# Gathers issued in five bursts, a new order in the last pair, and one-hots of two tables per comparison, in a DLRM tower kernel

## The chip, the cores and the metric

The kernel runs on one core of a Trainium2 chip. The metric is the device time of one execution in microseconds (us), lower is better. In the profile the engines are PE (TensorE's matmuls), PEld (TensorE's weight loads), DVE (VectorE), ACT (ScalarE), POOL (GpSimd) and SP (SyncE).

## The reference, cut to what matters

For each of 2048 samples, 27 embeddings of 128 values are looked up in 27 tables, all pairs of them are multiplied (351 dot products), 16 context values are appended, and three dense layers follow.

```python
e = jnp.stack([tbl_0[ids[:, 0]], ..., tbl_26[ids[:, 26]]], axis=1)   # 2048 x 27 x 128
z = (e @ e^T)[:, i < j]                                              # 2048 x 351
h = concatenate([z, dense_ctx], axis=1)                              # 2048 x 367
h = maximum(h @ W_top1 + b_top1, 0)                                  # 512
h = maximum(h @ W_top2 + b_top2, 0)                                  # 256
y = h @ W_top3                                                       # 1
```

The tables have 1,000 to 125,000 rows. All is float32.

## The kernel before

The samples go in 8 pairs `p` of two tiles `t` of 128 samples. Pair 0 and pair 7 are written out, pairs 1 to 6 are one hardware loop (`sweep`). Every engine has its own program in that form, and semaphores tie them together.

The embeddings come in two ways. Ten tables of 1000 rows and one of 1250 stay in SBUF (`parts`, `x_parts`) and are looked up by matmul: VectorE makes one-hot columns by comparing the ids with row numbers (`make_onehot`, line 591, eight comparisons of 256 columns for one table), TensorE multiplies table and one-hot (`lookup`, line 697, two tables `k` at a time, five lookups of 32 matmuls; `lookup_x`, line 713). There are four one-hot buffers (`OH = 4`), so a one-hot waits until TensorE is through with the one four before it (`slot_free`). Semaphore `s_looked` counts first tables of a lookup, `emb_filled` counts finished PSUM banks.

The other 16 tables (numbers `n` = 0 to 15) are gathered by GpSimd: an indirect DMA per table and tile brings 128 rows (line 418), 32 gathers a pair (`x_rows` adds two in pair 0). They wait one for another (`one_queued`), for their buffer, and for a point of TensorE's program given by `keep_step`, which is asked once for each group of four. TensorE transposes the rows (`transpose_rows`, line 733), ScalarE or VectorE move them to `embT` (lines 463 to 471 and 597).

TensorE's order in pair `p` of the loop is: lookup 0, transpose of z of the pair before (tile 1), lookups 1 and 2, half of the first layer of the pair before (line 760), lookups 3 and 4, `lookup_x`, transposes of tile 0, rest of the first layer, gram 0, transposes of tile 1, second layer (line 774), gram 1, third layer (line 782), transpose of z of tile 0. A gram (`gram`, line 741) is 128 small matmuls, each a product of one sample's embeddings with themselves, which show as 256 matmul records and 256 weight loads. VectorE then turns the result (`flip`, line 603) and lays out z (`fill_z`). In pair 7 the dense layers of the last pair itself come in smaller steps (`LAST_LAYERS`, `last_rows`, lines 799 to 812).

The points that gathers wait for in the loop are, by groups of four: tile 0, n 0 to 3 none beyond the buffer; n 4 to 7 the end of tile 0's transposes of the pair before; n 8 to 11 its gram 0; n 12 to 15 its last transposes of tile 1. Tile 1: n 0 to 3 its gram 1; then the ends of lookups 0, 1 and 2 of this pair.

## Time and profile before

| | us |
|---|---|
| median of 3 runs (576.52 to 586.41) | 583.2 |
| profiled execution, its own time | 578.39 |
| its span in the profile | 576.6 |
| PE busy | 400.8 |
| DVE busy | 279.8 |
| POOL busy | 289.7 |
| mean granted TensorE clock | 0.828 of full |

The sums of the prediction are made against the profiled execution (578.39), which lies within the runs' spread and 0.8% under their median.

### The profile page before, as it was taken

To read this page: it belongs to the slowest core of one execution; us is meant where nothing else is said; L and a number is where in the kernel's file an instruction comes from. 1 tells how busy PE (TensorE), PEld (TensorE's weight loads), DVE (VectorE), ACT (ScalarE), POOL (GpSimd) and SP (SyncE) were. 2 spreads that over 40 slices of the span, in tenths; PEclk is the share of its full clock that TensorE was granted. 3 is DMA by queue.
4 is the path that set the end of the run, shared out by engine and by line. 5 is a ranking of instruction groups with operands and counts; after the bars stand their busy time and mean duration, and the time that the engine had idled before them with its cause. 6 is when DMAs were issued, how large, how long until landed. Compare 5 with 4: busy or idle time off the path is not lost.

```text
span 576.6 us, 15362 instructions
## 1 busy us (share of the span) xinstructions
PE 400.8 (70%) x6218; PEld 358.6 (62%) x6218; DVE 279.8 (49%) x804; ACT 142.1 (25%) x189; POOL 289.7 (50%) x264
## 2 busy tenths in 40 slices
PE   2756357877697365985778965796669926894865
PEld 2745347766596264875677853785549915794655
DVE  5673168774185341664427932555237904390210
ACT  2673111231132220222212411123102402132221
POOL 6673555534387553345426444484435974395000
PEclk9887558996798676888888977897679978798997
DMA  8984322121113112122121311221113221101000
GB/s 193 273 202 120 106 54 60 40 89 34 34 42 105 42 36 67 22 65 70 35 64 40 95 32 34 54 88 42 33 34 80 77 51 32 29 16 41 2 3 0
DMA packets 22295, 36.58 MB, mean 63 GB/s; under 512 B 12662, under 2 KB 13310, under 8 KB 22252
## 3 DMA queue, kind: packets, MB, share of 16 engines
q1 hardware_dynamic: 13996, 19.01, 12.1%
q0 software_dynamic: 8256, 16.92, 11.5%
q8 instruction: 36, 0.59, 0.4%
q14 instruction: 7, 0.06, 0.0%
HBM read 35.90 MB, written 0.01 MB: 62 GB/s over the span
## 4 chain that ended last, share of the span: by engine, by line
PE 58%; issue 25%; DVE 7%; another core or an unknown queue 5%; ACT 3%; DMA 2%; SPq 1%; DVEq 0%
PE emb_ps L697 22%; PE gram_ps L741 13%; PE emb_ps L733 5%; DVE onehot L591 5%; PE mlp_ps L760 5%; PE mlp_ps L774 4%; PE emb_ps L713 3%; DMA embT<-in_tbl 2%; PE mlp_ps L803 1%; PE mlp_ps L782 1%; PE mlp_ps L751 1%; PE mlp_ps L808 1%; ACT onehot L452 1%; DVE turned L603 1%
## 5 line engine op out<-in xcount | busy, mean ns | idle before, releaser
L418 POOL DMA_INDIRECT rows<-in_tbl,idx x256 | 287.3, 1122 | 238.2 <-PE gram_ps L741 81.8
L591 DVE TENSOR_SCALAR onehot<-ids_b,row_of 128x256 fp32r<-128x256 int32 x694 | 200.4, 365 | 69.1 <-remote 37.3
L697 PE MATMUL emb_ps<-onehot,parts 125*128 125x256 f32 x1280 | 177.4, 298 | 40.5 <-issue 37.9
L697 PEld LDWEIGHTS emb_ps<-onehot,parts 125*128 125x128 f32 x1280 | 168.6, 203 | 46.4 <-issue 43.0
L741 PE MATMUL gram_ps<-embT 128*32 128x26 f32 x4096 | 78.5, 223 | 103.0 <-issue 93.0
L741 PEld LDWEIGHTS gram_ps<-embT 128*32 128x32 f32 x4096 | 65.2, 144 | 119.8 <-issue 117.0
L603 DVE STREAM_TRANSPOSE turned<-gram_ps 128x832 f32<-128x832 f32 x16 | 16.8, 1050 | 149.3 <-PE gram_ps L741 149.3
L463 ACT ACTIVATE embT<-emb_ps 128x512 f32<-128x512 f32 x40 | 48.9, 1224 | 147.5 <-PE emb_ps L697 72.4
L471 ACT ACTIVATE embT<-emb_ps 128x512 f32<-128x512 f32 x32 | 36.9, 1226 | 105.1 <-PE emb_ps L733 94.1
L597 DVE COPY embT<-emb_ps 128x512 f32<-128x512 f32 x32 | 35.9, 1180 | 53.0 <-remote 29.4
L733 PE MATMUL emb_ps<-ident,rows 128*128 128x128 f32 x256 | 39.2, 312 | 13.0 <-ACT embT L467 11.6
L733 PEld LDWEIGHTS emb_ps<-ident,rows 128*128 128x128 f32 x256 | 34.5, 164 | 14.5 <-ACT embT L467 12.1
L760 PE MATMUL mlp_ps<-zT,w_sb 128*128 128x256 f32 (+1 forms) x168 | 42.5, 404 | 0.2 <-issue 0.2
L760 PEld LDWEIGHTS mlp_ps<-zT,w_sb 128*128 128x128 f32 (+1 forms) x168 | 33.4, 206 | 5.4 <-issue 0.6
L482 ACT ACTIVATE h<-mlp_ps,b_sb 128x256 f32<-128x256 f32 x42 | 17.5, 468 | 48.1 <-PE mlp_ps L760 15.6
L774 PE MATMUL mlp_ps<-h,w_sb 128*128 128x256 f32 x112 | 25.5, 379 | 0.9 <-issue 0.9
L713 PE MATMUL emb_ps<-onehot,x_parts 125*128 125x256 f32 x140 | 20.8, 299 | 5.5 <-issue 5.2
L713 PEld LDWEIGHTS emb_ps<-onehot,x_parts 125*128 125x128 f32 x140 | 19.3, 203 | 6.4 <-issue 6.3
L774 PEld LDWEIGHTS mlp_ps<-h,w_sb 128*128 128x128 f32 x112 | 20.7, 190 | 3.6 <-issue 1.0
L489 ACT ACTIVATE y<-mlp_ps 1x256 f32<-1x256 f32 x7 | 2.6, 374 | 61.6 <-PE mlp_ps L782 61.6
L475 ACT ACTIVATE zT<-mlp_ps 128x384 f32<-128x384 f32 x14 | 7.4, 526 | 14.2 <-PE mlp_ps L751 14.0
L618 DVE COPY z<-turned 128x351 f32<-128x351 f32 x16 | 9.4, 588 | 1.8 <-issue 0.2
(43 smaller groups left out, 112.7 us busy)
## 6 DMA issues: line engine op xcount, KB each, us to landing
ids_b<-in_ids_mm SPq DMA_DIRECT2D x8, 896.0 KB
ids_b<-in_ids_mm SPq DMA_DIRECT2D x16, 256.0 KB
rows<-in_tbl,idx POOLq DMA_INDIRECT x256
embT<-in_tbl SPq DMA_DIRECT2D x6, 448.0 KB
w_sb<-in_tbl SPq DMA_DIRECT2D x2, 448.0 KB
turned<-in_tbl SPq DMA_DIRECT2D x1, 560.0 KB
w_sb<-in_W_top SPq DMA_DIRECT2D x1, 512.0 KB, 4.7
turned<-in_tbl SPq DMA_DIRECT2D x1, 448.0 KB
```

Of the source, the lines that this page charges most:

```text
L418: pool.indirect_dma_start(rows[:, t, n, :], None, tables[f], bass.IndirectOffsetOnAxis(idx[:, t, f:f + 1], 0), engine_sem=gathers_written) ...
L463: nc.scalar.activation(*lookup_views(k), ACT.Copy).then_inc(emb_act, 1)
L471: nc.scalar.activation(*row_views(t, k), ACT.Copy).then_inc(emb_act, 1)
L591: last = nc.vector.tensor_scalar(onehot[:, k % OH, c, :], ids_b[:, of, :], row_of[:, first + c:first + c + 1], None, ALU.is_equal)
L597: nc.vector.tensor_copy(*row_views(t, k)).then_inc(emb_dve, 1)
L603: nc.vector.transpose(turned[:, 0:NJ * G], gram_ps[:].rearrange("p (g j) -> p j g", g=G)[:, 0:NJ, :]).then_inc(s_turned, 1)
L697: last = nc.tensor.matmul(emb_ps[BANK[k]][:, m * W:(m + 1) * W], parts[0:MP, f, part, c * D:(c + 1) * D], onehot[0:MP, f % OH, c, :], star ...
L713: last = nc.tensor.matmul(emb_ps[BANK[XJOB]][:, 0:W], x_parts[0:MP, part, at:at + D], onehot[0:MP, (NM + h) % OH, c, :], start=(h == part ...
L733: done = nc.tensor.transpose(bank[:, m * P:(m + 1) * P], rows[:, t, n, :], ident[:])
L741: last = nc.tensor.matmul(gram_ps[q * COLS:(q + 1) * COLS, g * COLS:g * COLS + NJ], embT[:, t, at:at + COLS], embT[:, t, at:at + NJ], star ...
L760: done = nc.tensor.matmul(mlp_ps[job % 2][:, m * W:(m + 1) * W], w1_sb[0:K1[c], c, n * P:(n + 1) * P], zT[0:K1[c], c, :], start=(c == 0), ...
L774: done = nc.tensor.matmul(mlp_ps[0][:, m * W:(m + 1) * W], w2_sb[:, n, m * P:(m + 1) * P], h1[:, n, :], start=(n == 0), stop=(n == N1 - 1))
```

## The change

Four things are changed. `keep_step` is asked before each gather, and waits at five places of a pair only, so that the 32 gathers run in bursts of 4, 7, 7, 7 and 7: tile 0's n 0 to 3 wait for gram 0 of the pair before; n 4 to 10 for its gram 1; tile 0's n 11 to 15 with tile 1's n 0 and 1 for the first table of lookup 1; tile 1's n 2 to 8 for the first half of the first layer; n 9 to 15 for the first table of lookup 4. Pair 0 has steps of its own. In pair 7 the order is z and transposes, then half of h1, half of gram 1, the other halves, h2; `LAST_LAYERS` follows that. After pair 0, `make_two` makes the one-hots of two tables with eight comparisons of 512 columns, and signals both at their end; it waits for both buffers at once.

```diff
-LAST_LAYERS = [(kind, t) for t in range(TILES) for kind in ("z", "h1", "h2", "y")]
+LAST_LAYERS = [("z", 0), ("h1", 0), ("h2", 0), ("z", 1), ("y", 0), ("h1", 1), ("h2", 1), ("y", 1)]
...
-            def keep_step(p, t, k):
+            def keep_step(p, t, n):
                 if isinstance(p, int) and p == 0:
...
+                    if (t, n) == (0, 8):
+                        pool.wait_ge(s_looked, looked(p, 0))
+                    elif (t, n) == (0, 13):
+                        pool.wait_ge(s_looked, looked(p, 1))
+                    elif (t, n) == (1, 0):
+                        pool.wait_ge(s_looked, looked(p, 2))
+                    elif (t, n) == (1, 5):
+                        pool.wait_ge(s_looked, looked(p, 3))
+                    elif (t, n) == (1, 10):
+                        pool.wait_ge(s_looked, looked(p, 4))
+                    else:
+                        return
+                elif (t, n) == (0, 0):
+                    pool.wait_ge(gram_filled, (p - 1) * TILES + 1)
+                elif (t, n) == (0, 4):
                     pool.wait_ge(gram_filled, p * TILES)
+                elif (t, n) == (0, 11):
+                    pool.wait_ge(s_looked, looked(p, 1))
+                elif (t, n) == (1, 2):
+                    pool.wait_ge(mlp_filled, (p - 1) * MLP_JOBS + 3)
+                elif (t, n) == (1, 9):
+                    pool.wait_ge(s_looked, looked(p, LOOK - 1))
                 else:
-                    pool.wait_ge(emb_filled, p * JOBS + k)
+                    return
                 pool.sem_inc(pool_waited, 1)
...
-                        keep_step(p, t, k)
                         for n in TR[k]:
                             f = GATHERED[n]
+                            keep_step(p, t, n)
                             one_queued((p * TILES + t) * NG + n + (TILES if first and t else extra))
...
+            def make_two(p, k):
+                dve.wait_ge(s_ids[ids_part(k)], (p + 1) * 16)
+                if k >= OH:
+                    slot_free(dve, p, k + 1 - OH)
+                else:
+                    held = NM if isinstance(p, int) and p == 1 else NE
+                    slot_free(dve, p - 1, [e for e in range(held) if e % OH == k + 1][-1])
+                for c in range(CH):
+                    last = nc.vector.tensor_scalar(onehot[:, k % OH:k % OH + LOOK_TABLES, c, :],
+                                                   ids_b[:, k:k + LOOK_TABLES, :], row_of[:, c:c + 1], None,
+                                                   ALU.is_equal)
+                last.then_inc(s_onehot, LOOK_TABLES)
...
                 if not first:
-                    for k in range(OH, NE):
-                        make_onehot(p, k)
+                    for k in range(OH, NM, LOOK_TABLES):
+                        make_two(p, k)
+                    for h in range(XHALVES):
+                        make_half(p, h)
                 if not last and not first:
-                    make_onehot(p + 1, 0)
-                    make_onehot(p + 1, 1)
+                    make_two(p + 1, 0)
...
-                    if not last and not first:
-                        make_onehot(p + 1, 2 + t)
+                    if not last and not first and t == 0:
+                        make_two(p + 1, LOOK_TABLES)
                     flip(p, t)
...
                 transpose_rows(p, 1, 1)
                 third_layer(p - 1)
                 last_layers("z", 0)
-                last_layers("h1", 0)
-                last_layers("h2", 0)
                 transpose_rows(p, 1, 2)
                 transpose_rows(p, 1, 3)
-                last_layers("y", 0)
+                last_layers("h1", 0, range(0, N1 // 2))
+                gram(p, 1, range(0, G // 2))
+                last_layers("h1", 0, range(N1 // 2, N1))
+                gram(p, 1, range(G // 2, G))
+                last_layers("h2", 0)
...
             sweep(pe, body)
-            for kind, t in LAST_LAYERS[4:]:
+            for kind, t in LAST_LAYERS[3:]:
                 last_layers(kind, t)
```

`make_half` is the old `make_onehot` for the two halves of the 1250-row table. ScalarE's program follows the same order.

## Rows read from the trace of the kernel before

**Rows 1.** The page, section 1: busy us, share of the span, instructions

```profile
PE 400.8 (70%) x6218; PEld 358.6 (62%) x6218; DVE 279.8 (49%) x804; ACT 142.1 (25%) x189; POOL 289.7 (50%) x264
```

**Rows 2.** The page, section 4: the chain that ended last, by engine

```profile
PE 58%; issue 25%; DVE 7%; another core or an unknown queue 5%; ACT 3%; DMA 2%; SPq 1%; DVEq 0%
```

**Rows 3.** Windows from a gram's start to its end: length, busy times, clock, DMA

```profile
125.10:136.74 11.64, 5.78 (x258) 4.29 (x258) 1.05 (x4) 0.84 (x2) 5.42 (x6) 0.68 0.16 42
...
461.41:480.94 19.53, 6.32 (x258) 4.96 (x258) 0.98 (x4) 0.84 (x2) 10.49 (x12) 0.65 0.17 41
...
sum 137.86, PE 62.78 PEld 51.70 DVE 16.28 ACT 9.35 POOL 59.54; mean PE 5.23 PEld 4.31 DVE 1.36 ACT 0.78 POOL 4.96
```

**Rows 4.** The same view: gram 0 of pair 7

```profile
536.86:539.22 2.36, 2.36 (x258) 2.32 (x258) 0.00 (x0) 0.84 (x2) 0.00 (x0) 1.00 0.03 7
```

**Rows 5.** Windows of pairs 1 to 6, gram 1's end to the next one's

```profile
356.78:431.11 74.33, 52.72 (x775) 46.46 (x774) 33.14 (x102) 15.29 (x19) 40.08 (x32) 0.81 0.19 50
...
sum 407.88, PE 295.38 PEld 265.15 DVE 207.97 ACT 88.73 POOL 214.83; mean PE 49.23 PEld 44.19 DVE 34.66 ACT 14.79 POOL 35.80
```

**Rows 6.** Windows of pairs 1 to 6, gram 1's end to gram 0's start

```profile
sum 234.87, PE 197.45 PEld 182.46 DVE 160.70 ACT 65.61 POOL 132.31; mean PE 32.91 PEld 30.41 DVE 26.78 ACT 10.93 POOL 22.05
```

**Rows 7.** Timelines of POOL and PE around gram 0 of pair 4

```profile
326.88 0.95 POOL L418 DMA_INDIRECT rows<-in_tbl,idx  x1 [6.75 <-PE emb_ps L733]
328.13 0.95 POOL L418 DMA_INDIRECT rows<-in_tbl,idx  x1 [0.30 <-DMA rows<-in_tbl,idx]
...
335.63 0.95 POOL L418 DMA_INDIRECT rows<-in_tbl,idx  x1 [0.30 <-issue]
342.20 0.95 POOL L418 DMA_INDIRECT rows<-in_tbl,idx  x1 [5.62 <-PE gram_ps L741]
...
329.65 0.54 PE L741 MATMUL gram_ps<-embT 128*32 128x26 f32 x39
...
338.35 2.87 PE L741 MATMUL gram_ps<-embT 128*32 128x26 f32 x205 [0.46 <-issue]
```

**Rows 8.** Windows of two runs of gathers, each cut where TensorE slows

```profile
243.57:251.56 7.99, 7.99 (x58) 7.60 (x57) 6.31 (x21) 2.13 (x4) 6.16 (x7) 1.00 0.18 47
...
342.20:347.00 4.80, 4.75 (x57) 3.95 (x55) 4.65 (x12) 2.27 (x4) 3.78 (x4) 1.00 0.17 41
...
251.56:254.99 3.43, 0.91 (x3) 0.52 (x4) 0.71 (x3) 0.00 (x0) 1.40 (x2) 1.00 0.19 48
```

**Rows 9.** Timeline of lookups beside gathers, pair 4

```profile
300.29 7.82 PE L697 MATMUL emb_ps<-onehot,parts 125*128 125x256 f32 x64
...
302.86 0.97 POOL L418 DMA_INDIRECT rows<-in_tbl,idx  x1 [2.09 <-remote]
...
314.34 11.94 DVE L591 TENSOR_SCALAR onehot<-ids_b,row_of 128x256 fp32r<-128x256 int32 x42 [3.62 <-remote]
...
314.50 1.21 ACT L463 ACTIVATE embT<-emb_ps 128x512 f32<-128x512 f32 x1 [8.88 <-remote]
```

**Rows 10.** Timeline of a gather beside one-hots, pair 5

```profile
367.65 12.17 DVE L591 TENSOR_SCALAR onehot<-ids_b,row_of 128x256 fp32r<-128x256 int32 x46
...
369.94 10.00 POOL L418 DMA_INDIRECT rows<-in_tbl,idx  x1 [7.48 <-PE emb_ps L697]
```

**Rows 11.** Windows of pair 0's grams and of pair 7

```profile
58.30:73.15 14.85, 5.83 (x257) 5.00 (x258) 1.49 (x1) 0.92 (x1) 7.57 (x8) 0.50 0.32 99
73.15:88.51 15.36, 8.59 (x274) 7.75 (x274) 9.02 (x22) 2.37 (x2) 7.72 (x8) 0.51 0.21 53
496.39:536.86 40.47, 32.71 (x230) 29.62 (x228) 20.64 (x64) 10.85 (x13) 25.55 (x16) 0.90 0.12 28
539.22:561.23 22.01, 15.15 (x339) 12.38 (x339) 4.25 (x6) 5.81 (x13) 0.00 (x0) 1.00 0.01 2
```

**Rows 12.** Timeline of the end, pair 7's gram 1 and h1

```profile
548.01 2.94 PE L803 MATMUL mlp_ps<-zT,w_sb 128*128 128x128 f32 x24 [0.58 <-ACT zT L497]
...
565.00 5.12 PE L803 MATMUL mlp_ps<-zT,w_sb 128*128 128x128 f32 x24 [0.58 <-ACT zT L497]
```

More of the change, by code:

```diff
@@ L544, in body @@
                                 layers(p - 1, 4)
-                                for kind, t2 in LAST_LAYERS[:3]:
-                                    last_layers(kind, t2)
+                                last_layers("z", 0)
                             move_rows(p, t, k)
-                    if last and t:
-                        last_layers(*LAST_LAYERS[3])
-                    elif not first:
+                    if not first and not (last and t):
                         layers(p - 1, 2 + t)
@@ L559, in _ @@
             sweep(act, body)
-            for kind, t in LAST_LAYERS[4:]:
+            for kind, t in LAST_LAYERS[1:]:
                 last_layers(kind, t)
@@ L577, in split_x_low, with make_onehot, make_half @@
                                         x_parts[0:MP, 0, :].bitcast(F32), ALU.subtract).then_inc(s_x_low, 1)
[L579 to L582 removed]
+            def make_onehot(k):
+                dve.wait_ge(s_ids[ids_part(k)], 16)
                 if k >= OH:
[L584 to L592 removed]
+                    slot_free(dve, 0, k - OH)
+                for c in range(CH):
+                    last = nc.vector.tensor_scalar(onehot[:, k % OH, c, :], ids_b[:, k, :], row_of[:, c:c + 1], None,
+                                                   ALU.is_equal)
+                last.then_inc(s_onehot, 1)
+            def make_two(p, k):
[3 more added lines that the diff above has]
+                else:
+                    held = NM if isinstance(p, int) and p == 1 else NE
+                    slot_free(dve, p - 1, [e for e in range(held) if e % OH == k + 1][-1])
+                for c in range(CH):
+                    last = nc.vector.tensor_scalar(onehot[:, k % OH:k % OH + LOOK_TABLES, c, :],
+                                                   ids_b[:, k:k + LOOK_TABLES, :], row_of[:, c:c + 1], None,
+                                                   ALU.is_equal)
+                last.then_inc(s_onehot, LOOK_TABLES)
+            def make_half(p, h):
+                slot_free(dve, p, NM + h - OH)
+                for c in range(XH):
+                    at = CH + h * XH + c
+                    last = nc.vector.tensor_scalar(onehot[:, (NM + h) % OH, c, :], ids_b[:, NM, :],
+                                                   row_of[:, at:at + 1], None, ALU.is_equal)
                 last.then_inc(s_onehot, 1)
@@ L734, in transpose_rows, with gram @@
                 done.then_inc(emb_filled, 1)
-            def gram(p, t):
-                past(pe, s_turned, p * TILES + t)
-                for g in range(G):
+            def gram(p, t, gs=range(G)):
+                if 0 in gs:
+                    emb_moved(p, t)
+                    past(pe, s_turned, p * TILES + t)
+                for g in gs:
                     for q in range(Q):
@@ L743, in gram @@
                                                 start=True, stop=True)
-                last.then_inc(gram_filled, 1)
+                if G - 1 in gs:
+                    last.then_inc(gram_filled, 1)
             def transpose_z(p, t):
@@ L784, in third_layer, with last_layers @@
                 done.then_inc(mlp_filled, 1)
-            def last_layers(kind, t):
+            def last_layers(kind, t, ns=range(N1)):
                 job, cols = LAST_LAYERS.index((kind, t)), bass.ts(t, P)
@@ L800, in last_layers @@
                 elif kind == "h1":
-                    for n in range(N1):
+                    for n in ns:
                         for c in range(KCH):
@@ L864, in body @@
                                 calls += 1
-                    emb_moved(p, t)
-                    gram(p, t)
+                        gram(p, t)
                 if not first and not last:
@@ L872, in _ @@
             sweep(pe, body)
-            for kind, t in LAST_LAYERS[4:]:
+            for kind, t in LAST_LAYERS[3:]:
                 last_layers(kind, t)
```

42 lines of the change are left out of this document (8 added, 34 removed).

## The prediction

> **What bounds the kernel now.** I read the page's busy shares first [rows 1]: TensorE is busy 70% of the span, no other engine over 50%. The chain that ended last [rows 2] is 58% TensorE and 25% "issue", that is, TensorE waiting for nothing that the profile shows. So the question is where TensorE, with work in hand, doesn't run. Windows laid on the grams answer it. The twelve grams of pairs 1 to 6 take 137.86 us, 11.5 each [rows 3]; the one gram that has no gather beside it, in pair 7, does the same 256 matmuls and 256 weight loads in 2.36 us [rows 4].
>
> The timelines of GpSimd and TensorE, side by side, show what is different. Gathers start every 1.25 us (326.88, 328.13). Eight of them run from 326.88 to 335.63 + 0.95 = 336.58. Gram 0 starts at 329.65, gets through 39 matmuls in 0.54 us, then almost stops until 338.35, where the other 205 go in 2.87 us [rows 7]. The next gathers start at 342.20, 1.0 us after that gram's end. Windows cut at the slowing give it a size [rows 8]: from the first gather of a burst on, TensorE gets through 58 + 57 records of lookups in 8.0 us in one case, and 57 + 55 of transposes, dense layer and gram in 4.8 us in the other; after that it makes 3 + 4 records in 3.4 us, until 254.99, 1.7 us after the end of the last of eight gathers (243.57 + 8 x 1.25 - 0.30 = 253.27). Five more bursts give counts of 53 to 63 each. So a burst costs TensorE nothing for its first 115 to 130 records, and nearly everything from there to 1.7 us after its end. Lookups need 7.6 us for 120 records, a gram less than one. That is why eight gathers are cheap beside lookups and dear beside a gram.
>
> A burst also keeps TensorE's signals back. The lookup that ends at 308.11 (300.29 + 7.82) is seen by ScalarE at 314.50 and the one-hots that wait for its first half start at 314.34, both 1.8 us after the burst's end (302.86 + 9.7 = 312.56); GpSimd's own condition is held too, so that bursts with a condition met meanwhile stand 2.09 us apart [rows 9].
>
> A pair takes 407.88 / 6 = 68.0 us [rows 5]: 234.87 / 6 = 39.1 from gram 1 to the next gram 0, the lookups above all [rows 6]; 23.0 in the two grams; the rest, (407.88 - 234.87 - 137.86) / 6 = 5.9, transposes of tile 1 and second layer.
>
> **The change part by part.** *Bursts, grams.* No condition lets a burst start just before gram 0; only the burst of four, which starts 1.0 us after gram 0, is near gram 1. Gram 0: 2.4 us. Gram 1: the four gathers start at +1.0 after gram 0, end at 1.0 + 4 x 1.25 - 0.3 = +5.7, let TensorE go at +7.4. TensorE reaches gram 1 at +5.9 with about 50 records made since the burst's start, makes 70 of 512, and the rest after +7.4 in 2.0: end +9.4, so gram 1 takes 3.5. Grams and what is between: 2.4 + 9.4 = 11.8 in place of 23.0 + 5.9 = 28.9, a gain of 17.1 a pair.
>
> *Bursts, lookups.* This is the cost. 28 gathers instead of mostly 16 now stand between gram 1 and gram 0, in four bursts of 7 x 1.25 - 0.3 = 8.45 us, more than the 7.6 us that TensorE has for free in lookups. The conditions are met while the burst before still runs (lookup 0 and a table of lookup 1 are 48 matmuls of 7.82 / 64 = 0.122 us [rows 9], 5.9, with some 2 us of third layer and transposes before them; the burst of seven ends at +9.5), so the next starts 2.1 us after its end. The chain is 1.0 + 4 x 8.45 + 3 x 2.1 = 41.1, + 1.7 until TensorE is let go, + 1.2 for the last move of transposed rows (the size of ScalarE's move in [rows 9]): 44.0. TensorE's own work there is 32.9 of 39.1 [rows 6], so GpSimd's chain ends later and sets it. Gathers back to back, without the 2.1s, would give 1.0 + 34.7 + 1.7 + 1.2 = 38.6, the lower bound.
>
> Two things come on top. *One-hots in twos*: same columns, same VectorE time if the time goes by columns: 46 comparisons of 256 columns take 12.17 us [rows 10], 0.264 each, so 0.53 for 512. But the first table of a lookup is signalled eight comparisons of 256, 2.1 us, later, and the one-hots now wait for a whole lookup. Behind the waiting comparison on VectorE are the other one-hots, the next moves of rows and `flip`; TensorE's next lookup waits for all. While VectorE is ahead by four buffers this is covered; after a burst that held the signals it isn't: 120 records are just the four buffers. I take 3 us a pair (one and a half such starts), 0 to 8 as ends (four starts). *Blocked gathers*: the gather at 369.94 takes 10.00 us while one-hots run without a break from 367.65 to 379.82 [rows 10]; there are four such (10.0 to 13.7 us) in the trace. Meanwhile TensorE runs free, as at 369.06. In the new chain GpSimd has less slack. 4 x 10.6 / 6 = 7 us a pair if all of it counts, 0 if none; I take 2, as the conditions behind it are then met and the gaps go.
>
> The stretch is then 44 + 3 + 2 = 49 in place of 39.1, a loss of 9.9. A pair: 49 + 11.8 = 60.8 against 68.0, 7.2 less; six pairs: -43.
>
> *Pair 0* [rows 11]. Gram 0 of 14.85 us loses its eight gathers (the steps of pair 1 wait for its end) but the last burst of pair 0 now starts later, so I leave it 3: -12. From there to gram 1's end 15.4 becomes 9.4: -6.
>
> *Pair 7* [rows 11]. Its stretch of 40.47 becomes 49: +8.5; gram 0 was clean already. The new order puts the last transposes into the wait for ScalarE's zT and h1 and the gram into the waits around it: the chain from gram 0's end to gram 1's end, 22.0 us, loses h2 (16 matmuls, 16 x 2.94 / 24 = 2.0 us), y, and the waits of TensorE for h1, h2 and the moved rows: between -2 and -8, I take -5. H1 of tile 1 takes 5.12 at the end against 2.94 earlier [rows 12], its clock granted at half after a wait; -1 for a part of that. Sum -6.
>
> Sum: 578.4 - 43 - 18 + 8.5 - 6 = 520 us, 10% under the profiled time.
>
> **Two rules of the Trainium skill.** The row of one-hots shows 0.264 us for 256 columns [rows 10]. The Trainium skill, VectorE: DVE Perf Modes, section on the TRN2 errata, says that operations from SBUF pay a fixed cost per instruction, 58 cycles, and should be 512 elements or wider. By that rule, 40 comparisons fewer would save an estimated 2.4 us of VectorE a pair, and the sum would be some 515; start to start, the trace shows no such cost. The same group shows a gather blocked through a run of one-hots. The Trainium skill, SBUF — State Buffer, section "Who interferes with whom", says that a VectorE instruction with one SBUF input, outside the two-port modes, doesn't contend with GpSimd. By that rule the blocks would not come, and the stretch would be 47, the sum 506; the trace disagrees with the 10.00 us.
>
> **The rivals.** *The bursts are covered* (12%). The stretch stays at about 39 to 43: TensorE's 120 free records reach nearly through a burst, and half a first layer in a burst, with fewer records per us, stretches them. For it: clean bursts of four, and pair 6 did the stretch in 461.41 - 431.11 = 30.3 us [rows 3, 5]. Against it: GpSimd's chain of 38.6 to 44.0 is there in any case. At 41: 6 x 8 less, 520 - 48 - 8 = 464.
>
> *Holds cost more than they free, but not all* (18%). Each of four holds is followed by one-hots that start from empty buffers (2.1 to 4.3 us) and by lookups at half clock. Stretch 53 to 57: +6 us for each of seven, 520 + 42 = 562.
>
> *The blocked gather becomes the bound* (10%, the other side). A gather that meets a run of one-hots waits for the run's end. Now bursts start just as VectorE gets its signals back, so each of three bursts in the lookups can meet one, and comparisons are twice as long. At 10.6 us and no cover, the stretch is 44 + 3 + 10.6 n for n blocks a pair. The gain of 17.1 is used up at a stretch of 56.2, n = 0.9; with n = 1.4 it is 62, a pair takes 74, and the whole 520 + 7 x 13 = 611. It decides from about one counted block a pair; the trace has 0.6, mostly covered. Pair 5, with one, is the longest at 74.33 [rows 5]; pair 6, with one, has a gram of 19.5 us [rows 3].
>
> *The conditions don't hold the gathers off the grams* (part of the above): if the last burst starts later than its point, gram 0 waits for its end. This costs nothing beyond the 44.0, which already waits for it.
>
> **How the numbers follow.** The forecast, stretch of 44 to 53, gives 485 to 548 and has 60%. The rivals have 12, 18 and 10. The range of 474 to 566 leaves out about half of the first and all of the last, with a little between. A difference under 2% can't be told from none here. Faster by over 2% (under 571.5): 0.60 + 0.12 + most of 0.18 = 0.84. Within 2%: 0.09. Slower by over 2%: 0.07.
>
> **What the profile of the changed kernel would show.** Gram 0 at 2.4 to 5 us and gram 1 at 3 to 5 in pairs 1 to 6. Gathers in runs of 4, 7, 7, 7, 7 with 2.1 us between. The time from gram 1 to gram 0 at 44 or more, its end set by the last burst. TensorE stopping in lookups some 7.6 us into a burst, then VectorE's one-hots starting 1.7 us after the burst. One-hots of 512 columns 0.53 us apart. Wrong would be: grams still at 10 us; gathers of 10 us twice in each pair; a stretch over 56.

## The result, and the profile after

| | before, us | after, us |
|---|---|---|
| median of the runs | 583.1 (576.5 to 586.4) | 509.0 (506.3 to 517.7) |
| profiled execution, its own time | 578.39 | 506.26 |
| its span | 576.6 | 504.3 |

The ratio is 0.875, 95% interval 0.864 to 0.885: faster by 12.5%. The profiled execution lost 72.1 us. All of this holds for the chip on which both kernels were measured here. On the one other chip on which the whole change was timed, the kernel before takes 431 us and the change makes it 12 us (3%) slower, and half of the experiments are about that.

The page after, sections 1 and 4 (engine busy times; the chain that ended last, by engine), answers to [rows 1] and [rows 2]:

```profile
PE 384.9 (76%) x6218; PEld 347.5 (69%) x6218; DVE 236.6 (47%) x524; ACT 142.7 (28%) x189; POOL 273.0 (54%) x264
PE 57%; issue 15%; another core or an unknown queue 13%; DVE 6%; DMA 3%; ACT 3%; SPq 1%; DVEq 0%
```

Waiting for nothing visible ("issue") fell from 25% to 15% of the chain. Waits put down to "another core or an unknown queue" rose from 5% to 13%: the kernel runs on one core, and in the timeline below such waits (there `remote`) are signals that arrive late. VectorE's work fell by 43.2 us with 280 comparisons fewer.

Windows of pairs 1 to 6. First the grams, two of the twelve and the sum [rows 3, 4]:

```profile
111.51:116.21 4.70, 2.99 (x257) 2.57 (x258) 2.85 (x8) 0.84 (x2) 0.24 (x1) 1.00 0.08 21
...
175.53:177.88 2.35, 2.35 (x257) 2.31 (x258) 2.35 (x8) 0.00 (x0) 0.00 (x0) 1.00 0.06 6
...
sum 52.50, PE 34.05 PEld 31.19 DVE 14.42 ACT 8.38 POOL 9.53; mean PE 2.84 PEld 2.60 DVE 1.20 ACT 0.70 POOL 0.79
```

Then from one gram 1's end to the next one's [rows 5], and from gram 1's end to gram 0's start [rows 6]:

```profile
127.66:186.70 59.04, 45.97 (x776) 42.13 (x774) 27.36 (x62) 14.94 (x19) 34.36 (x32) 0.91 0.21 61
...
sum 356.07, PE 283.14 PEld 258.03 DVE 169.82 ACT 88.76 POOL 206.13; mean PE 47.19 PEld 43.01 DVE 28.30 ACT 14.79 POOL 34.36
...
69.20:111.51 42.31, 34.49 (x227) 32.08 (x227) 24.04 (x58) 10.78 (x12) 29.89 (x28) 0.85 0.27 77
...
sum 271.26, PE 216.79 PEld 198.69 DVE 130.53 ACT 67.02 POOL 176.94; mean PE 36.13 PEld 33.11 DVE 21.75 ACT 11.17 POOL 29.49
```

The grams gave back 137.86 - 52.50 = 85.4 us; the stretches between took 271.26 - 234.87 = 36.4 more; what is left of the pairs gained 2.8. Six pairs: -51.8.

The timeline of the burst of seven after gram 1 of pair 1 shows the price (start, length, engine, line, work; in brackets the idle time before it and what ended it; [rows 7, 9, 10] are its like before):

```profile
128.65 0.94 POOL L427 DMA_INDIRECT rows<-in_tbl,idx  x1 [6.74 <-PE gram_ps L766]
128.77 4.03 PE L720 MATMUL emb_ps<-onehot,parts 125*128 125x256 f32 x32
...
132.89 2.02 PE L720 MATMUL emb_ps<-onehot,parts 125*128 125x256 f32 x15
...
135.80 0.64 PE L720 MATMUL emb_ps<-onehot,parts 125*128 125x256 f32 x4 [0.89 <-issue]
...
137.27 0.52 PE L720 MATMUL emb_ps<-onehot,parts 125*128 125x256 f32 x3 [0.83 <-issue]
...
138.78 6.42 DVE L605 TENSOR_SCALAR onehot<-ids_b,row_of 128x512 fp32r<-128x512 int32 x16 [8.79 <-remote]
...
139.92 1.05 POOL L427 DMA_INDIRECT rows<-in_tbl,idx  x1 [2.83 <-remote]
...
141.27 4.05 POOL L427 DMA_INDIRECT rows<-in_tbl,idx  x1 [0.30 <-issue]
142.09 5.56 PE L720 MATMUL emb_ps<-onehot,parts 125*128 125x256 f32 x32 [2.05 <-DVE onehot L605]
```

TensorE stops at 134.9, 6.3 us into the burst. The burst ends at 137.09 (its last gather starts at 136.15 and takes 0.94), VectorE and GpSimd get their signals 1.7 and 2.8 us later, and TensorE then waits 2.05 us for two whole tables of one-hots. The gather beside those one-hots takes 4.05 us and ends with them (141.27 + 4.05 = 145.32; 138.78 + 6.42 = 145.20).

Where a burst is still running when gram 0 is due, gram 0 pays. In pair 2 the last gather has ended (171.95 + 0.94) and gram 0 starts 2.6 us later; in pair 4 gram 0 starts with the last two gathers still to end, and takes 5.22 us:

```profile
171.95 0.94 POOL L427 DMA_INDIRECT rows<-in_tbl,idx  x1 [0.30 <-issue]
...
291.48 0.43 PE L766 MATMUL gram_ps<-embT 128*32 128x26 f32 x27
292.58 1.28 POOL L427 DMA_INDIRECT rows<-in_tbl,idx  x1 [0.30 <-issue]
293.12 0.18 PE L766 MATMUL gram_ps<-embT 128*32 128x26 f32 x1 [1.21 <-issue]
...
294.55 2.15 PE L766 MATMUL gram_ps<-embT 128*32 128x26 f32 x227 [0.53 <-issue]
```

Windows of pair 7's stretch, its gram 0, from there to gram 1's end, and the rest [rows 11, 12]:

```profile
425.27:470.20 44.93, 36.79 (x231) 32.76 (x228) 17.44 (x40) 12.01 (x15) 28.13 (x28) 0.89 0.17 42
470.20:475.15 4.95, 2.78 (x257) 2.62 (x257) 0.00 (x0) 0.00 (x0) 0.00 (x0) 0.93 0.03 7
475.15:491.44 16.29, 13.99 (x322) 11.77 (x320) 4.24 (x6) 5.15 (x10) 0.00 (x0) 0.92 0.01 2
491.44:504.30 12.86, 8.62 (x67) 7.22 (x67) 2.09 (x4) 3.41 (x11) 0.00 (x0) 1.00 0.00 1
```

### The profile page after: what moved, and what is told of

It is laid out like the page before. It is cut to its first block, busy times and chain, and to the rows that moved or that the text cites. A ratio compares the mean times of both kernels' runs of the same rounds, so it can differ in the third digit from the quotient of the medians.

```text
span 504.3 us, 15021 instructions
## 1 busy us (share of the span) xinstructions
PE 384.9 (76%) x6218; PEld 347.5 (69%) x6218; DVE 236.6 (47%) x524; ACT 142.7 (28%) x189; POOL 273.0 (54%) x264
## 4 chain that ended last, share of the span: by engine, by line
PE 57%; issue 15%; another core or an unknown queue 13%; DVE 6%; DMA 3%; ACT 3%; SPq 1%; DVEq 0%
PE emb_ps L720 25%; PE gram_ps L766 10%; PE mlp_ps L786 6%; PE emb_ps L756 5%; PE mlp_ps L800 5%; PE emb_ps L736 4%; DMA embT<-in_tbl 3%; DVE onehot L605 3%; DVE turned L627 1%; DVE embT L621 1%; PE mlp_ps L829 1%; SPq L272 1%; ACT onehot L461 1%; PE mlp_ps L777 0%
## 5 line engine op out<-in xcount | busy, mean ns | idle before, releaser
L427 POOL DMA_INDIRECT rows<-in_tbl,idx x256 | 270.7, 1058 | 192.0 <-PE gram_ps L766 68.9
L720 PE MATMUL emb_ps<-onehot,parts 125*128 125x256 f32 x1280 | 195.5, 309 | 66.4 <-issue 48.1
L720 PEld LDWEIGHTS emb_ps<-onehot,parts 125*128 125x128 f32 x1280 | 179.9, 212 | 76.8 <-issue 56.8
L605 DVE TENSOR_SCALAR onehot<-ids_b,row_of 128x512 fp32r<-128x512 int32 x280 | 114.8, 485 | 77.3 <-remote 46.1
L766 PE MATMUL gram_ps<-embT 128*32 128x26 f32 x4096 | 48.8, 199 | 36.8 <-issue 27.0
L766 PEld LDWEIGHTS gram_ps<-embT 128*32 128x32 f32 x4096 | 43.7, 116 | 45.3 <-issue 40.4
L615 DVE TENSOR_SCALAR onehot<-ids_b,row_of 128x256 fp32r<-128x256 int32 x70 | 21.9, 379 | 57.6 <-remote 51.7
L756 PE MATMUL emb_ps<-ident,rows 128*128 128x128 f32 x256 | 35.3, 293 | 3.5 <-ACT embT L476 3.1
L736 PE MATMUL emb_ps<-onehot,x_parts 125*128 125x256 f32 x140 | 27.4, 360 | 6.8 <-issue 6.6
L736 PEld LDWEIGHTS emb_ps<-onehot,x_parts 125*128 125x128 f32 x140 | 25.5, 271 | 9.8 <-issue 9.8
L591 DVE TENSOR_SCALAR onehot<-ids_b,row_of 128x256 fp32r<-128x256 int32 x64 | 20.2, 386 | 5.3 <-DMA ids_b<-in_ids_mm 5.3
```

The source lines that it names most:

```text
L427: pool.indirect_dma_start(rows[:, t, n, :], None, tables[f], bass.IndirectOffsetOnAxis(idx[:, t, f:f + 1], 0), engine_sem=gathers_written) ...
L605: last = nc.vector.tensor_scalar(onehot[:, k % OH:k % OH + LOOK_TABLES, c, :], ids_b[:, k:k + LOOK_TABLES, :], row_of[:, c:c + 1], None, A ...
L615: last = nc.vector.tensor_scalar(onehot[:, (NM + h) % OH, c, :], ids_b[:, NM, :], row_of[:, at:at + 1], None, ALU.is_equal)
L720: last = nc.tensor.matmul(emb_ps[BANK[k]][:, m * W:(m + 1) * W], parts[0:MP, f, part, c * D:(c + 1) * D], onehot[0:MP, f % OH, c, :], star ...
L736: last = nc.tensor.matmul(emb_ps[BANK[XJOB]][:, 0:W], x_parts[0:MP, part, at:at + D], onehot[0:MP, (NM + h) % OH, c, :], start=(h == part ...
L756: done = nc.tensor.transpose(bank[:, m * P:(m + 1) * P], rows[:, t, n, :], ident[:])
```

## The experiments

Each later kernel was timed beside the kernel before on its own chip, and the first thing seen was that the kernel before takes 430 us on five chips and 570 on two. The table gives medians in us, and the chip by its number.

| label | chip | before | kernel | ratio, 95% interval |
|---|---|---|---|---|
| e1_bursts_only | 11 | 430.1 | 438.4 | 1.020 (1.009 to 1.030) |
| e2_wide_only | 11 | 430.1 | 426.9 | 0.995 (0.987 to 1.004) |
| e3_order_only | 11 | 430.1 | 421.9 | 0.984 (0.978 to 0.990) |
| e5_twos_of_256 | 11 | 430.1 | 428.7 | none given |
| e0_after (the change itself) | 12 | 431.4 | 443.3 | none given |
| e6_no_gathers | 12 | 431.4 | 387.1 | none given |
| e4_after_single_tables | 1 | 432.3 | 422.4 | 0.980 (0.967 to 0.993) |
| e7_one_burst_of_28 | 1 | 432.3 | 437.0 | 1.013 (1.003 to 1.024) |
| e8_order_and_wide | 10 | 431.7 | 420.4 | 0.973 (0.965 to 0.980) |
| e10_bursts_only_again | 0 | 430.1 | 440.9 | 1.026 (1.016 to 1.035) |
| e9_no_wait_for_gram_1 | 13 | 568.7 | 558.4 | 0.981 (0.975 to 0.988) |
| e11_no_wait_for_gram_1_again | 15 | 571.5 | 556.7 | 0.972 (0.960 to 0.983) |

Three medians say less than they seem to. On chip 12 one of eleven runs of the kernel before took 414.6 us and the others 427.4 to 434.6. One run of e5 took 416.4 and the other three 428.0 to 429.5; its trace is of the 416.4. The four runs of e10 lie between 431.2 and 455.7; its trace is of the 431.2.

### One part of the change at a time

e1_bursts_only is the kernel before with the new `keep_step` alone:

```diff
-                        keep_step(p, t, k)
                         for n in TR[k]:
                             f = GATHERED[n]
+                            keep_step(p, t, n)
```

> The kernel before with the five bursts alone. Theory A (the gain is gathers taken off the grams): 515 to 530 us, grams of pairs 1 to 6 at 2.4 to 6 us, the stretch from gram 1 to gram 0 at 45 to 48. Rival B (the wide comparisons carry a large part): 545 us or more, the grams short all the same.

e2_wide_only is the kernel before with `make_two` and `make_half` alone:

```diff
-                    for k in range(OH, NE):
-                        make_onehot(p, k)
+                    for k in range(OH, NM, LOOK_TABLES):
+                        make_two(p, k)
```

> The kernel before with the one-hots of two tables alone. Theory A: 575 to 585 us, within 2% of before, since the grams stay at 10 to 12 us. Rival B: 560 or less.

e3_order_only is the kernel before with the new `LAST_LAYERS` and `last_rows` alone:

```diff
-LAST_LAYERS = [(kind, t) for t in range(TILES) for kind in ("z", "h1", "h2", "y")]
+LAST_LAYERS = [("z", 0), ("h1", 0), ("h2", 0), ("z", 1), ("y", 0), ("h1", 1), ("h2", 1), ("y", 1)]
```

> The kernel before with the new order of the last pair alone. Theory A: 5 to 9 us less than before in the span after gram 0 of pair 7, so 574 to 578 in all. Rival B: nothing, because the last chain is set by gram 1 and h1 of tile 1.

e5_twos_of_256 is the changed kernel with each comparison of 512 columns as two of 256, the signal still for two tables:

```diff
-                for c in range(CH):
-                    last = nc.vector.tensor_scalar(onehot[:, k % OH:k % OH + LOOK_TABLES, c, :],
-                                                   ids_b[:, k:k + LOOK_TABLES, :], row_of[:, c:c + 1], None,
+                for m in range(LOOK_TABLES):
+                    for c in range(CH):
+                        last = nc.vector.tensor_scalar(onehot[:, k % OH + m, c, :], ids_b[:, k + m, :],
+                                                       row_of[:, c:c + 1], None,
```

> The kernel after, but each comparison of 512 columns made as two of 256; both tables are still signalled together. The trace after shows 0.396 us from one 512-wide comparison to the next, 0.263 for 256 before, that is 0.13 fixed and 0.52 ns a column. Theory C (the width counts): one-hots of two tables take 4.2 us in place of 3.2, and TensorE waits for them after each burst, some three starts a pair: 520 to 530 us. Rival D (only the number of signals or the burst holds count): 506 to 512.

The times expected for all four were those of a chip like the first, and all four missed: on this one the kernel before took 430.1 us. What they show is what the parts are worth where a gram isn't stopped. Windows of the grams of pairs 1 to 6 in e3_order_only, whose gathers stand where they stood before:

```profile
148.88:152.76 3.88, 3.51 (x258) 2.92 (x258) 1.04 (x4) 0.84 (x2) 2.96 (x4) 1.00 0.19 53
...
sum 55.94, PE 41.91 PEld 35.23 DVE 15.20 ACT 10.10 POOL 42.50; mean PE 3.49 PEld 2.94 DVE 1.27 ACT 0.84 POOL 3.54
```

There are 42.50 us of gathers beside them, where [rows 3] had 59.54, and still a gram takes 4.7 us and not 11.5; one with four gathers beside it takes 3.88. So there four gathers beside a gram cost some 1.5 us together (3.88 - 2.36), and the bursts have little to gain: alone they lose 2%, the order alone gains 8 us, the wide one-hots 3, which can't be told from nothing (the interval goes from a gain of 6 to a loss of 2).

### Is it the chip, and is it the gathers?

e0_after is the changed kernel unaltered, to see it on such a chip.

> The changed kernel itself, beside the kernel before once more. On the chip of the four runs so far the kernel before takes 430 us, and its grams take 3.8 to 6 us with gathers beside them. Theory E (a burst of gathers holds TensorE on some chips only, and the change pays there alone): where before takes 575 to 590, after takes 500 to 520; where before takes 425 to 435, after takes 420 to 440, since the bursts cost 8 us there, the order gains 7 and the wide comparisons 2. Rival F (the hold is there on every chip, and the 430 us have another cause): a ratio of 0.86 to 0.89 wherever it runs.

e6_no_gathers is the kernel before with the gathers and the loads of their indices left out after pair 0. TensorE transposes pair 0's rows again in every pair, so 7 of 8 pairs compute with the wrong embeddings for 16 of the 27 tables.

```diff
                 extra = 0 if first else TILES
+                if not first:
+                    return
...
-                        load_idx(p + 1, t)
...
-                pe.wait_ge(s_rows[t][k], (p + 1) * 16 * len(TR[k]))
+                pe.wait_ge(s_rows[t][k], 16 * len(TR[k]))
```

> The kernel before, with all gathers and index loads left out after pair 0 (TensorE transposes the rows of pair 0 again, so the results of later pairs are not the reference's). Theory E: where before takes 575 to 590, this takes 400 to 420, all grams of pairs 1 to 6 at 2.4 to 5 us; where before takes 430, it takes 390 to 415. Rival F: about 410 in both.

On chip 12 the changed kernel took 443.3 us and the kernel before 431.4: the two differ by 12 us, the other way than at first, so the rival that expected 0.86 to 0.89 everywhere is out. (Both kernels fell just outside what had been expected: 443.3 against 420 to 440, 387.1 without gathers against 390 to 415.) The changed kernel's pairs, from one gram 1's end to the next, sum to 311.36 us against 356.07 on the first chip, and 18 of the 45 us lie in TensorE's busy time, at a granted clock of 0.90 to 0.94 against 0.86 to 0.92; the other 27 are stops that aren't there. Without gathers the pair is 247.56 / 6 = 41.3 us and every gram in the loop from pair 2 on takes 2.35 or 2.36. So even here the gathers of the kernel before cost 431 - 387 = 44 us, and on the first chip nearly 200, if the rest takes as long there.

The gathers themselves don't tell the chips apart. Their packets of 4096 bytes took 248 ns on average in the kernel before on the first chip, 247 in e3_order_only on chip 11; 240 in e9_no_wait_for_gram_1 on chip 13 and 238 in e0_after on chip 12. On each of the seven chips all runs of the kernel before are of one kind, but for one single run of 518 us on chip 1, at a granted clock of 0.653, of which there is no trace. But each of the seven was used in one sitting only, and the number of the first chip isn't known. So whether the kind belongs to the chip, or to something that lasts for a sitting, wasn't tried; "chip" in this text stands for both. What makes the difference isn't shown by any of these runs.

### What costs the change 12 us on the other chips

e4_after_single_tables is the changed kernel with the old one-hots, one table at a time (bursts and order alone). e7_one_burst_of_28 is the changed kernel without the three conditions within the lookups, so that after gram 1 all gathers go one behind the other.

```diff
-                elif (t, n) == (0, 11):
-                    pool.wait_ge(s_looked, looked(p, 1))
-                elif (t, n) == (1, 2):
-                    pool.wait_ge(mlp_filled, (p - 1) * MLP_JOBS + 3)
-                elif (t, n) == (1, 9):
-                    pool.wait_ge(s_looked, looked(p, LOOK - 1))
```

> The kernel after with one-hots of one table per comparison and per signal, as before: bursts and order alone. Where before takes about 430 us (gathers don't hold TensorE): bursts alone took 438 and the order alone 422, so 430 by the sum of parts; theory G (the wide comparisons cost time there, because one signal for two tables and a wait for both buffers delay the lookup) says 425 to 432, under the 443 of the whole; rival H (the bursts are what costs, the width nothing) says 438 to 445. Where before takes about 583 us: 505 to 520.

> The kernel after without the three conditions inside the lookups: after gram 1 the 28 gathers go in one run, held by their buffers alone. Where gathers hold TensorE (before at 583): after 115 to 130 records TensorE would stop until the run ends, 28 us later, so the stretch from gram 1 to gram 0 is 60 or more and the whole 600 or more. Where they don't (before at 430): the last rows of tile 1 land earlier, TensorE doesn't wait for them, and the whole is 425 to 435, under the 443 of the kernel after.

e8_order_and_wide is the kernel before with both parts other than the bursts.

> The kernel before with two of the three parts of the change, the order of the last pair and the one-hots of two tables; the gathers keep their old places. If TensorE waits for gathered rows only because the bursts start them after gram 1 (theory A), this kernel shows no idle time of TensorE put down to the gathers' DMA, as the wide one-hots alone and the order alone didn't, and the two gains add: 430 - 8 - 3, so 416 to 424 us where the kernel before takes 430. If it is the wide comparisons themselves that cost, by stretching the gathers beside them and by asking for two free buffers at once (theory B), the sum of the gathers' time grows as in the whole change and the time is 430 to 440. On a chip where gathers hold TensorE, as in the first measurement (the kernel before at 583), the gathers would stand in both grams as before, and only the tail and pair 7 would be shorter: 560 to 580.

The list of TensorE's waits shows the cause in one line. In e0_after, e7_one_burst_of_28 and e4_after_single_tables it has this wait of the transposes for gathered rows (us in total, times, longest):

```profile
PE emb_ps L756 <- DMA rows<-in_tbl,idx: 21.8, 9, 4.3
```

```profile
PE emb_ps L749 <- DMA rows<-in_tbl,idx: 17.7, 6, 4.5
```

```profile
PE emb_ps L739 <- DMA rows<-in_tbl,idx: 5.4, 5, 2.4
```

In e1_bursts_only it is 13.6, in e10_bursts_only_again 15.5, in e5_twos_of_256 3.0. In e2, e3 and e8, with the gathers at their old points, there is no such wait.

Windows of pairs 1 to 6 show where the time goes. In e0_after the six stretches up to gram 0 take 197.84 us and the twelve grams 48.25, both less than in e3_order_only (201.92 and 55.94). What is left, from gram 0's end to gram 1's start, where tile 1 is transposed, takes 65.27 against 32.83: the whole loss and more.

The trace of e0_after shows why: after gram 1 of pair 0 (end at 67.73) GpSimd starts 32 gathers from 68.70 to 111.30 without a pause, the first 28 for pair 1. In pairs 2, 4 and 6 the last of these 28 starts 37.5 to 38.8 us after gram 1 (mean spacing 1.35 to 1.40 us). TensorE is at gram 0 after 29.88 us in its quickest pairs (223.85 to 253.73), done with it at 33.5, and would be at the last transposes 1.3 us after that (as in pair 3 of e7, which waits for nothing there). In pair 4 these start 40.1 us after gram 1, 2.6 us after the start of the last of the 28. The rows come late. After such waits the clock falls too: the second layer behind them, in the window 108.90 to 114.70, has a granted clock of 0.71.

e7 took 437.0 us and missed the 425 to 435 expected: with all gathers in one run the rows still come late. The conditions within the lookups cost little, and in two pairs only: in pairs 3 and 5 of e0_after GpSimd reaches the first of them before it is met and waits 7.1 and 7.3 us:

```profile
184.44 0.94 POOL L427 DMA_INDIRECT rows<-in_tbl,idx  x1 [7.13 <-PE emb_ps L720]
```

e7 has no such pause, no wait for rows in these two pairs, and is 4 us shorter in them. e8 says that without the bursts nothing is lost: 416 to 424 had been expected if the late start of the gathers is the cause, 430 to 440 if the wide comparisons were; it took 420.4.

But the wide comparisons make it worse. GpSimd's groups of gathers (count, busy us, mean ns), of e0_after and of e4_after_single_tables:

```profile
L427 POOL DMA_INDIRECT rows<-in_tbl,idx x256 | 264.4, 1033 | 148.5 <-DMA rows<-in_tbl,idx 66.0 <-PE gram_ps L766 52.0 <-PE emb_ps L720 17.2
```

```profile
L427 POOL DMA_INDIRECT rows<-in_tbl,idx x256 | 245.7, 960 | 143.8 <-DMA rows<-in_tbl,idx 60.5 <-PE gram_ps L749 38.7 <-PE emb_ps L703 21.7
```

A gather takes 1033 and 1043 ns (e0, e7) beside comparisons of 512 columns and 960 and 963 (e4, e5) beside those of 256, all four with the bursts. That is 32 x 73 ns = 2.3 us a pair on the engine that is the bound there: in e4's pairs 2, 4 and 6 the last of the 28 gathers starts 35.0 to 36.4 us after gram 1. Against e0, TensorE waits 16 to 19 us less for rows in all. e5 has the one signal for two tables and the wait for both buffers, as the changed kernel has, so by one trace of each it is the width that counts and not these.

With the bursts, narrow comparisons are the better choice by some 15 us on one chip (e4 at 422.4 against 437.0 of e7, which also lacks the three conditions) and by 15 to 21 across chips (422 and 429 against 443). e4 beat both forecasts (425 to 432, 438 to 445). But e1 and e10 have the narrow comparisons as well, and the same loop as e4, and wait 13.6 and 15.5 us for rows; less the 8 us of the order they would be at 430 and 433. About half of these waits (8.7 and 7.0 us) is in one pair each, the one in which a single gather takes 8.46 and 8.63 us. So narrow comparisons don't keep the rows in time by themselves, and the gain lies between 10 and 21 us. Without bursts, where GpSimd has slack, e2 and e8 show no harm of the wide ones, though their gathers take 1020 and 1034 ns too.

### One wait, on the chips where gathers stop TensorE

e9_no_wait_for_gram_1 is the changed kernel without the second burst's condition:

```diff
-                elif (t, n) == (0, 4):
-                    pool.wait_ge(gram_filled, p * TILES)
```

> The whole changed kernel with one of its waits left out: the gathers of a pair still start after gram 0 of the pair before, but the second burst no longer waits for gram 1, so gathers stand beside gram 1 and the rows are begun some 8 us earlier. If rows gathered too late are what the bursts cost where gathers don't hold TensorE (theory A), TensorE's idle time put down to the gathers' DMA, 21.8 us in the changed kernel, falls to under 5 us, gram 1 takes some 1.5 to 3 us longer, and the time is 420 to 430 us beside 430 of the kernel before and 443 of the change. If the wide one-hots or the bursts' later waits cost it (theory B), it stays at 438 to 445. On a chip where gathers hold TensorE, gram 1 would grow from 3.5 to some 11 us and the time would be 520 to 550 us.

It fell on chip 13, where the kernel before takes 568.7. It took 558.4, where 520 to 550 had been expected: 2% of a gain in place of 12.5%. Gram windows of pairs 1 to 6, two and the sum; then the same from gram 1's end to the next one's:

```profile
192.36:195.68 3.32, 2.77 (x258) 2.46 (x258) 2.65 (x7) 0.84 (x2) 0.03 (x1) 1.00 0.11 24
200.97:215.22 14.25, 5.51 (x258) 4.64 (x258) 0.00 (x0) 0.84 (x2) 7.01 (x8) 0.60 0.15 38
...
sum 113.91, PE 51.98 PEld 44.70 DVE 15.41 ACT 8.11 POOL 46.35; mean PE 4.33 PEld 3.72 DVE 1.28 ACT 0.68 POOL 3.86
...
sum 398.13, PE 296.69 PEld 265.78 DVE 168.82 ACT 89.79 POOL 191.34; mean PE 49.45 PEld 44.30 DVE 28.14 ACT 14.96 POOL 31.89
```

Gram 1, with eight or nine gathers beside it, takes 13.96 to 17.01 us, more than the 11 expected; gram 0 stays at 2.34 to 7.12. Against the whole change the six pairs are 42.1 us longer: +61.4 in the grams, -18.9 in the stretches, which have seven gathers fewer to cover. So this one wait is worth 7 us a pair, and without it the ratio is 0.98 (0.97 in the repetition) where the whole change has 0.875: some four fifths of the gain, though the two were measured on different chips.

e10_bursts_only_again was sent for such a chip and fell on another, where it repeats e1 in its median:

> The kernel before with the bursts alone, as in the second experiment, once more, on whichever chip it falls. By now both grams clear of gathers are my theory for the gain where gathers hold TensorE (the kernel before at 565 to 585), and that stands or falls with the bursts alone: there the pair should come to some 61 us, as in the whole change, pair 0 to end near 70, and with the old order of the last pair and the single one-hots the time to be 505 to 530, a ratio of 0.88 to 0.92. The rival gives the bursts no more than what they did in e9, 1 to 3 per cent, the rest being the order and the wide one-hots. On a chip where gathers don't hold TensorE (the kernel before near 430) it repeats 435 to 442, 1 to 3 per cent slower.

e11_no_wait_for_gram_1_again was sent for a chip where gathers don't stop TensorE and fell on chip 15, where they do; it repeats e9 (0.972 against 0.981):

> The whole change without the second burst's wait for gram 1, once more, for a chip on which gathers don't hold TensorE (the kernel before near 430). Theory A, that the wait for gram 1 makes the rows late there: TensorE's idle time put down to the gathers' DMA is under 5 us (21.8 in the whole change, 15.5 with the bursts alone), gram 1 stands beside gathers, and the time is 418 to 430, no slower than before. Theory B, that the later bursts' waits or the wide one-hots make them late: 435 to 445 and 15 us or more of such idle time. On a chip like the last one (before at 569) it repeats 555 to 560.

So two things stay open. What the bursts alone, without order and wide one-hots, give on such a chip wasn't measured; and on the others it wasn't tried whether dropping the wait for gram 1 takes the late rows away, though e8's missing wait for rows and the unbroken run of gathers speak for it.

## Why the prediction was right, and where it wasn't

The forecast was 520 us, and 509 was measured; against the profiled executions, -58 was forecast and -72 came. Term by term:

- *Grams.* Gram 0 was to be 2.4 and gram 1 3.5 us; they took 4.3 and 4.45 (means; 52.50 for the twelve). The mechanism is the one named: in pair 2, where the last burst ends 2.6 us before it, gram 0 takes 2.35. The trace shows three things in the extra. Gram 0 of pairs 4 to 6 starts before the last burst has ended (5.22, 5.03 and 5.35 us with two gathers beside each; the prediction had it wait for that end). The clock is low (3.18 us at 0.63, pair 3). And gram 1 of pairs 1 and 5 (6.16 and 5.88) stops for 2.4 and 2.2 us beside a packet of the instruction queue, of which the last section says more. Between the grams 5.9 was kept and 5.4 measured. Sum 14.1 against 11.8.
- *The stretch from gram 1 to gram 0.* Forecast 49, measured 271.26 / 6 = 45.2. The chain up to the last burst's end had been put at 41.1 us after gram 1, 46.1 with the 5 us for one-hots and blocked gathers. In the trace it ends after 42.6 to 48.0 us, 45.5 on average, so its length was right. Its parts were not: from pair 2 on there are two pauses in place of three (after gram 1 of pair 1 the third burst follows the second as one of 14, 139.92 to 160.67), but they are longer (2.8 and 3.3 us in this pair, 5.7 and 3.0 in pair 5), and come to 6.4 us a pair against 6.3. The step that was mis-sized is the last: from the burst's end to gram 0 2.9 us were added (1.7 + 1.2). Pairs 2 and 3 have 2.6. In the other four, gram 0 starts 0.2 to 2.5 us before the last burst's end. So the chain of bursts sets gram 0's start in two pairs, and in four TensorE is there first and pays in the gram.
- *The one-hots.* Here a step failed. I took time to go by columns, 0.53 us for 512, and wrote that start to start the trace shows no fixed cost. Sixteen comparisons of 512 took 6.42 us, 0.401 each, against 0.264 of 256 columns [rows 10]. The two together give about 0.13 us that doesn't depend on the width and 0.14 per 256 columns. A single width can't show a fixed cost, and I read an absence from it. The Trainium skill, VectorE: DVE Perf Modes, section on the TRN2 errata, says that there is such a cost, and the runs agree; they show more than the 2.4 us a pair that I had worked out from it, since 40 x 0.127 = 5.1. VectorE's busy time fell by 43.2 us. What the 3 us a pair for later signals should have been isn't measured on a chip like the first; in the burst shown above TensorE waits 2.05 us for one-hots.
- *Blocked gathers.* Taken at 2 us a pair, by 10.6 each. There are four of them of 4.05 us (141.27 the first, then one in each of pairs 3, 4 and 6), none of 10: each ends with the run of one-hots, and the run is now 16 comparisons of 0.4 and not 46 of 0.26. At 3.1 us over a gather's usual 0.94 they come to 2.1 us a pair, so the 2 that was taken was right by another sum: more of them counted, each cheaper. The rival that made this the bound fell with it. Of the other rule, the Trainium skill, SBUF — State Buffer, section "Who interferes with whom", the prediction said that the trace disagrees. That was a misreading: the rule frees instructions outside the two-port modes, and the same section counts this operation (a tensor with a scalar per row) among those that can enter one. The added 0.137 us per 256 columns are near an estimate of 0.133 from the table in the Trainium skill, VectorE: DVE Perf Modes, section on the TRN2 errata, with two columns a cycle. So the rule and the 4.05 us of the trace can stand together; the mode itself is in no row.
- *Together.* The stretch term of 49 was 3.8 too large, 3.2 of it in the step from the last burst's end to gram 0, and the grams with what is between them 2.3 too small. The two errors are partly one: where gram 0 didn't wait for the burst's end, it ran beside it. That they nearly cancel is luck. The pair came to 59.35 against 60.8, the six to -51.8 against -43 (68.0 was 7.2 over the forecast; it is 8.6 over the measurement).
- *Pair 0*: gram 1 ends at 69.20 and no longer at 88.51, -19.3 against -18.
- *Pair 7*: the stretch of 44.93 is +4.5 against +8.5, gram 0 +2.6 against 0; from gram 0's end to gram 1's 16.29 against 22.01, -5.7, and after that 12.9 against 15.4, -2.5; forecast -6 for both, measured -8.2. e3_order_only puts the order's part at 8 us where it stands alone, on a chip of the other kind.
- *Two readings of the rows.* The counts of records from a burst's start to TensorE's slowing add up to 109 to 124 in the seven cases, not 115 to 130; the 120 in the sums is within. And of the four blocked gathers before, the fourth is in pair 7, so that they come to 6 us a pair over seven, not 7 over six.
- *The sum*: -51.8 - 19.3 + 4.5 + 2.6 - 8.2 = -72.2, the 72.1 measured.

The rivals: the bursts aren't covered (the stretch grew by 6.1 us a pair, not 2), and the stretch isn't at 53 to 57. What no rival had is that the stop on which all rests was seen in three sittings of eight. That the forecast was made for one of these, and not for one of the five others, is luck. Where four gathers beside a gram cost 1.5 us, the bursts cost more than they free, through late rows, which no rival named either.

## What to carry to other kernels

Before an order of work is built round a contention, time the kernel on several chips. Here the kernel before takes 570 to 583 us in three measurements and 430 on five other chips, and the version that wins 12.5% on one chip loses 3% on one of the others. Order and wide one-hots without the bursts (e8) have the lowest ratio on the second kind, 0.973, though its interval overlaps those of e3 and e4 (0.984 and 0.980). A gate that holds transfers back is worth its cost only while the engine that issues them has time left: count transfers by their spacing against the stretch that remains, and take out of that engine's way what lengthens each transfer. And a row of one width says nothing of a fixed cost; only two widths do.

## What the runs showed of the hardware

*Stops in steps.* On the chips on which the kernel before takes 570 us a stopped TensorE doesn't stand still. In e9_no_wait_for_gram_1, timeline of gram 1 of pair 2:

```profile
200.97 0.52 PE L763 MATMUL gram_ps<-embT 128*32 128x26 f32 x37
202.35 0.26 PE L763 MATMUL gram_ps<-embT 128*32 128x26 f32 x3 [0.86 <-issue]
203.78 0.27 PE L763 MATMUL gram_ps<-embT 128*32 128x26 f32 x4 [1.17 <-issue]
205.19 0.30 PE L763 MATMUL gram_ps<-embT 128*32 128x26 f32 x2 [1.15 <-issue]
206.64 0.23 PE L763 MATMUL gram_ps<-embT 128*32 128x26 f32 x1 [1.14 <-issue]
207.34 0.20 PE L763 MATMUL gram_ps<-embT 128*32 128x26 f32 x1 [0.47 <-issue]
208.75 0.29 PE L763 MATMUL gram_ps<-embT 128*32 128x26 f32 x2 [1.21 <-issue]
...
212.30 2.92 PE L763 MATMUL gram_ps<-embT 128*32 128x26 f32 x201 [1.09 <-issue]
```

It goes on at multiples of 0.70 us, with one to four matmuls each time, until 2.2 us after the last gather's end (209.17 + 0.94). In the grams of pairs 0 to 6 of the kernel before, 109 matmuls start over 0.5 us after the one before them, 63 of these by 0.6 to 0.9 us and 36 by 1.3 to 1.6. This, and that a burst's first 109 to 124 records are free, looks like instructions that reach the engine in small portions while gathers' packets flow, after a stock has been used up. That is argued, not shown.

*Packets of the instruction queue.* On the other chips some pairs take 43 to 50 us and some 53 to 56, in e3_order_only in turn. The DMA queues of e3_order_only (packets, MB, share of the 16 engines) in the window 161.91 to 215.66, a pair of 53.75 us:

```profile
q0 software_dynamic: 1079, 2.19, 15.5%
q1 hardware_dynamic: 1266, 1.49, 8.8%
q8 instruction: 9, 0.15, 1.1%
```

In the pairs before and after it, of 42.90 and 44.31 us, there is no packet of the instruction queue, in the next long one (54.02) there are nine again. It is so in all nine traces with gathers on these chips: among pairs 2 to 6, those with nine packets take 53 us or more and are the longest of their kernel. The kernel alone doesn't set their number: e1 and e10 are one kernel and have two such pairs and one. e5_twos_of_256 has one in its trace of 416.4 us; its other three runs, of which there is no trace, took 12 us more. TensorE stops beside the packets. The first two of the nine start at 162.3 and 163.5, the third at 168.5:

```profile
166.59 2.47 PE L694 MATMUL emb_ps<-onehot,parts 125*128 125x256 f32 x13 [3.34 <-issue]
170.75 3.97 PE L694 MATMUL emb_ps<-onehot,parts 125*128 125x256 f32 x19 [1.68 <-issue]
```

Two more stops, of 1.3 and 2.0 us, stand beside later packets of this pair. The four, 8.2 us, are most of the 10. Gathers aren't needed for such stops: in e6_no_gathers no such packet comes between 110 and 314 us, and pairs 3 to 6 take 39.9 each, but pair 1 has ten packets, takes 46.6, and its gram 1 stops for 2.19 us beside the last of them:

```profile
111.83 0.26 PE L742 MATMUL gram_ps<-embT 128*32 128x26 f32 x7 [2.19 <-issue]
```

What decides in which pairs the packets come stays open. It bears on every comparison here of one trace with another: one such pair more or less is 10 us.
